# Film values of the modulated stage, made in two earlier stages of a four-layer cross-attention stack

## The chip, the cores and the metric

The kernel runs on one core of one Trainium2 chip. The metric is device time in microseconds (us); a lower one is better. A profile is one execution taken by the hardware profiler. In its rows PE is the tensor engine's matmuls, PEld its weight loads, DVE the vector engine, ACT the scalar engine, POOL the GpSimd engine, and SPq or ACTq a transfer (DMA) that SyncE or ScalarE issues. Every value is f32 unless a row says bf16.

## What is computed

The reference is a stack of four cross-attention layers, each followed by a feed-forward layer, on x of 32 batches x 256 rows x 256 columns and a context ctx of 32 x 120 x 192. The part around the change is in the fourth layer, cut here to what matters:

```python
V = x_vision @ Wv                      # x_vision is ctx; it depends on nothing computed before
c_t = einsum('btg,bgd->btd', attn_mean, V)
scale_in, shift_in = split(c_t @ W_film_in + b_film_in, 2)
...
y = s4d(x, ...)
scale_out, shift_out = split(c_t @ W_film_out + b_film_out, 2)
y = y * (1.0 + mod_gate * scale_out) + mod_gate * shift_out
xt = x_text + y                        # then a layer norm, a gelu feed-forward, a layer norm
```

Since c_t @ W_film_out is attn_mean @ (ctx @ (Wv @ W_film_out)), the kernel folds the two weights once (96 partitions x 2 x 512), makes "film values" of 120 x 512 from a batch's context, and multiplies them with the head weights attn_mean of the batch. ctx, Wv and W_film_out are inputs, so the film values can be made at any time.

## The kernel before

The stages, in the order in which they run, each over the 32 batches:

- a0, `heads_attention`: attention of the first layer. SyncE's queue loads per batch a "floor" of 2 x 960 KB beside the inputs. In its last four batches it also loads what `TernaryHeld` keeps for the next stage.
- one block of five parts that share the engines (`ternary_to_experts`): f0, the ternary feed-forward (`ternary_feed_forward`, tiles f_... and f0w_...); a1, attention; r, the routing; v, `film_rows`, which makes the 32 batches of film values for W_film_in and stores them in the tensor `films`; e, the experts.
- a2, `heads_attention` again, which loads what `AdaptiveHeld` keeps.
- fa, the gated feed-forward with the sparse attention of the fourth layer (`adaptive_with_sparse_attention`, tiles fa_...). It stores attn_mean as `head_weights`.
- cv, the convolution (`convolve_channels`), which loads what `ModulatedHeld` keeps.
- m3, the modulated feed-forward (`modulated_feed_forward`, tiles m_... and m3w_...), and behind it in the same block the low-rank feed-forward.

Between blocks stands a barrier over all engines. Inside a block each engine runs its instructions strictly in the order of the program. That order comes from slots: a part names steps with a lag, and in slot t each engine does, in the order of the list, step(t - lag) for every step whose batch exists. `run_parts` puts several parts side by side: in each slot first all steps of the first part, then those of the next. A part's `first` shifts it, `begin` says in which of its slots `start` runs. So whatever an early list entry waits for holds up everything behind it on that engine.

In f0, VectorE's `start` rounds two weight tiles of 128 x 2048 to ternary values. The mean of their absolute values needs a matmul with ones by TensorE (L1092). Then, for batch i, ScalarE's `norm` runs in slot i+2, TensorE's `turn` and `make_row` in slot i+3, `up` and `conv` in slot i+4 and `turn_max` in slot i+5. VectorE's `h_out` (L1000) empties `up` in slot i+4.

In m3, TensorE's list is `(6, up(0)), (2, film_values), (6, up(1)), (6, up(2)), (2, film_product), (6, up(3)), (5, turn_x), (7, down)`. `start` (L3261) folds the weights; `film_values` (L3270, m_v) makes one batch's values, ScalarE copies them out (L3248, m_vf), and `film_product` (L3279, m_f) multiplies them with the head weights. On VectorE `film_out` makes m_film of it, on POOL `mix` uses m_film.

```python
        def film_values(it):
            pe.wait_ge(c_in[it.p], 16 * (it.h + 1))
            if it.reused(1):
                pe.wait_ge(v_ready, it.i)
            for k in range(2):
                last = pe.matmul(v_ps[0:SK, :], cb[it.p][:, k, :], wvf[:, k, :], start=k == 0, stop=k == 1)
            last.then_inc(v_done, 1)
```

A matmul of this program stands in the trace as two PE instructions, so one batch of film values is x4 there.

Of the kernel before, what the change touches and what calls it, by code (L numbers as in the profile page):

```python
# [15 lines left out]
P = 128  # L16
# [803 lines left out]
def ternary_feed_forward(nc, const, src, dst, held, first, area):  # L820
# [37 lines left out]
    w_scale, w_all, sums, consts = (st.sem(n) for n in ("w_scale", "w_all", "sums", "consts"))  # L858
# [73 lines left out]
    def vector(dve):  # L932

        def start():
            for m, (wq, rows) in enumerate(((w1q, wf[0]), (w2q, wf[1]))):
                dve.tensor_reduce(wsum[:, m:m + 1], rows[:], AX.X, ALU.add, apply_absolute_value=True).then_inc(sums, 1)
                dve.wait_ge(w_all, 4 * m + 1)
                dve.tensor_scalar(wmean[:, m:m + 1], aux[:, 0:1], 1.0 / (D * H1), 1e-5, ALU.mult, ALU.max).then_inc(w_scale, 1)
# [4 lines left out]
                dve.wait_ge(w_all, 4 * m + 2)  # L943
                dve.tensor_scalar(rows[:], rows[:], MAGIC, 1.0, ALU.subtract, ALU.min).then_inc(w_all, 1)
                dve.wait_ge(w_all, 4 * m + 3)
                dve.tensor_scalar(wq[:].rearrange("p k n -> p (k n)"), rows[:], -1.0, 1.0 - 2.0 * m, ALU.max, ALU.mult).then_inc(w_all, 1)

            dve.wait_ge(w_all, 8)
            dve.tensor_reduce(wf[1][:, 0:D], w2q[:].rearrange("p k d -> p d k"), AX.X, ALU.add).then_inc(w_all, 1)
            dve.wait_ge(w_all, 9)  # L950
# [137 lines left out]
    def tensor(pe):  # L1088
        def start():
            for m in two:  # L1090
                pe.wait_ge(sums, m + 1)
                pe.matmul(aux[:, 0:1], const["ones"][:], wsum[:, m:m + 1], start=True, stop=True).then_inc(w_all, 1)  # L1092
            pe.wait_ge(w_all, 10)
# [59 lines left out]
        def down(it):  # L1153
# [11 lines left out]
            (3, make_row(aux, dg, dg_ready, row_done, row_ready)), (5, make_row(aux2, dg2, dg2_ready, row2_done, row2_ready)), (4, conv(1))], 4, start)  # L1165
    after = dict(turned=(turn_ready, B), row=(row_ready, B), hidden=(h_ready, 4 * B), conv=(silu_ready, KH * B), row2=(row2_ready, B), y=(y_ready, B), stored=stored)
# [3 lines left out]
def normed_attention(nc, const, src, dst, ctx, w, first, area, before):  # L1170
# [40 lines left out]
    def sync(sp):  # L1211
        def start():
# [2423 lines left out]
```

## Time and profile before

| | us |
|---|---|
| median of 3 runs | 4773.59 (4771.92 to 4776.9) |
| the profiled execution: its own time | 4771.23 |
| its span, first to last instruction | 4769.5 |
| PE busy | 4437.6 (93%) |
| PEld busy | 3454.4 (72%) |
| DVE busy | 3205.2 (67%) |
| ACT busy | 2043.9 (43%) |
| POOL busy | 2086.4 (44%) |
| mean granted clock of TensorE | 0.974 of full speed |

Busy time is the union of an engine's instructions over the span. Such a share is a mean over stages with different limits, so an edit has to be priced in its own stage: there the question is which engine never waits, and for what the others wait. The granted clock has two levels, 2.4 GHz (1.00 in the rows) and 1.2 GHz (0.50).

### The profile page before, as it was taken

To read this page: it belongs to the slowest core of one execution; us is meant where nothing else is said; L and a number is where in the kernel's file an instruction comes from. 1 tells how busy PE (TensorE), PEld (TensorE's weight loads), DVE (VectorE), ACT (ScalarE), POOL (GpSimd) and SP (SyncE) were. 2 spreads that over 40 slices of the span, in tenths; PEclk is the share of its full clock that TensorE was granted. 3 is DMA by queue.
4 is the path that set the end of the run, shared out by engine and by line. 5 is a ranking of instruction groups with operands and counts; after the bars stand their busy time and mean duration, and the time that the engine had idled before them with its cause. 6 is when DMAs were issued, how large, how long until landed. Compare 5 with 4: busy or idle time off the path is not lost. (4 is left out here: it accounts for less than half of the span.)

```text
span 4769.5 us, 90704 instructions
## 1 busy us (share of the span) xinstructions
PE 4437.6 (93%) x31788; PEld 3454.4 (72%) x31788; DVE 3205.2 (67%) x9688; ACT 2043.9 (43%) x4216; POOL 2086.4 (44%) x2505
## 2 busy tenths in 40 slices
PE   7999869999999999959999899999999978999999
PEld 5666647778776888846666688888888745777866
DVE  5888789987553333147777499999999944444444
ACT  3555447764443232224445344444444332222244
POOL 2222146543444233044443265665655503566532
PEclk9999989999999999979999899999999989999999
DMA  4666612235334322122222111111111073232233
GB/s 112 154 153 163 146 45 70 78 116 182 57 82 100 92 73 71 47 74 69 69 72 89 31 40 34 43 33 34 43 33 32 28 246 130 85 98 84 92 111 102
DMA packets 333274, 407.33 MB, mean 85 GB/s; under 512 B 58932, under 2 KB 294165, under 8 KB 322070
## 3 DMA queue, kind: packets, MB, share of 16 engines
q1 hardware_dynamic: 315190, 368.41, 27.3%
q0 software_dynamic: 13312, 25.25, 2.2%
q10 hardware_dynamic: 4320, 7.87, 0.6%
q8 instruction: 256, 4.19, 0.4%
q14 instruction: 196, 1.61, 0.1%
HBM read 304.45 MB, written 96.96 MB: 84 GB/s over the span
## 5 line engine op out<-in xcount | busy, mean ns | idle before, releaser
L2846 PE MATMUL fa_h<-fa_xnT,faw_w 128*128 128x256 f32 x2048 | 475.1, 383 | 0.0
L2858 PE MATMUL fa_y<-faw_w,fa_hT 128*128 128x256 f32 x2048 | 462.5, 379 | 0.0
L2858 PEld LDWEIGHTS fa_y<-faw_w,fa_hT 128*128 128x128 f32 x2048 | 386.5, 190 | 65.3 <-issue 15.4
L2846 PEld LDWEIGHTS fa_h<-fa_xnT,faw_w 128*128 128x128 f32 x2048 | 380.6, 191 | 56.5 <-issue 9.4
L2743 ACT ACTIVATE fa_hT<-fa_h,faw_b 128x256 f32<-128x256 f32 x512 | 215.0, 471 | 478.0 <-PE fa_h L2846 412.1
L531 DVE TENSOR_REDUCE a_mx<-a_score 128x16 f32<-128x1920 f32 x128 | 276.0, 2157 | 82.2 <-PE a_score L715 81.9
L1966 POOL DMA_INDIRECT e_xg<-moe_rows,e_idx x64 | 128.8, 2013 | 323.8 <-issue 244.7
L3241 ACT ACTIVATE m_hT<-m_h,m3w_b 128x256 f32<-128x256 f32 x256 | 107.5, 471 | 366.5 <-PE m_h L3301 366.5
L1716 PE MATMUL r_h<-r_xnT,r_rw 128*128 128x256 f32 x1024 | 250.1, 393 | 10.7 <-ACT r_hT L1667 10.7
L230 POOL TENSOR_SCALAR a_rs<-a_mv 128x2 f32<-128x2 f32 x96 | 21.4, 223 | 536.9 <-DVE a_mv L224 533.2
L2128 ACT ACTIVATE e_hT<-e_h,e_b 128x256 f32<-128x256 f32 x256 | 107.5, 471 | 329.5 <-PE e_h L2183 319.7
L3301 PE MATMUL m_h<-m_hnT,m3w_w 128*128 128x256 f32 x1024 | 237.5, 381 | 2.5 <-ACT m_hnT L3231 2.5
L3301 PEld LDWEIGHTS m_h<-m_hnT,m3w_w 128*128 128x128 f32 x1024 | 195.1, 191 | 54.2 <-issue 13.6
L2183 PE MATMUL e_h<-e_xT,e_w 128*128 128x256 f32 x1024 | 231.7, 380 | 0.9 <-DVE e_xT L1980 0.9
L2195 PE MATMUL e_y<-e_w,e_hT 128*128 128x256 f32 x1024 | 226.5, 379 | 0.0
L3311 PE MATMUL m_y<-m3w_w,m_hT 128*128 128x256 f32 x1024 | 226.4, 379 | 0.0
L1716 PEld LDWEIGHTS r_h<-r_xnT,r_rw 128*128 128x128 f32 x1024 | 189.6, 193 | 48.2 <-ACT r_hT L1667 23.8
L2195 PEld LDWEIGHTS e_y<-e_w,e_hT 128*128 128x128 f32 x1024 | 194.2, 190 | 26.4
L2183 PEld LDWEIGHTS e_h<-e_xT,e_w 128*128 128x128 f32 x1024 | 191.7, 190 | 25.8 <-DVE e_xT L1980 1.1
L3311 PEld LDWEIGHTS m_y<-m3w_w,m_hT 128*128 128x128 f32 x1024 | 192.1, 190 | 25.2 <-issue 0.4
L765 PE MATMUL a_av<-a_pT,a_vp 120*32 120x256 f32 x2048 | 180.9, 383 | 25.5 <-DVE a_qa L545 24.6
L2669 DVE MATCH_REPLACE8 fa_left<-fa_top,fa_left 128x120 f32<-128x120 f32 x768 | 195.4, 268 | 0.0
(453 smaller groups left out, 11063.3 us busy)
## 6 DMA issues: line engine op xcount, KB each, us to landing
a_floor<-a_lowest SPq DMA_DIRECT2D x64, 960.0 KB
cv_toep<-kernels SPq DMA_DIRECT2D x16, 2048.0 KB, 9.5
x<-a_xo SPq DMA_DIRECT2D x96, 256.0 KB, 3.2
f_xb<-x SPq DMA_DIRECT2D x64, 256.0 KB, 3.2
f_xres<-x SPq DMA_DIRECT2D x64, 256.0 KB, 3.0
a_xb<-x SPq DMA_DIRECT2D x64, 256.0 KB, 3.1
e_w<-in_L_ffn_ew SPq DMA_DIRECT2D x16, 1024.0 KB, 4.8
a_cb<-in_ctx SPq DMA_DIRECT2D x96, 90.0 KB, 2.1
```

What stands on the lines that cost most here:

```text
L531: c.add(dve.tensor_reduce(m, s_in, AX.X, ALU.max))
L765: pe.matmul(av[g * 32:(g + 1) * 32, m * S:(m + 1) * S], vp[it.at][:, (m * G + g) * E + e, :], pT[m][:, g, h * S:(h + 1) * S], start=h == 0 ...
L1716: last = pe.matmul(h_ps[m % 2][:, c, :], rw1[:, k, f:f + P], xnT[it.p][:, k, :], start=k == 0, stop=k == KD - 1)
L1966: pool.indirect_dma_start(xg[p][:, t, :], None, xn_all[:, :], bass.IndirectOffsetOnAxis(ap=idx[p][:, t:t + 1], axis=0), bounds_check=B * S ...
L2183: last = pe.matmul(h_ps[m][:, c, :], w1[e][:, k, f:f + P], xT[it.p][:, k, :], start=k == 0, stop=k == KD - 1)
L2195: last = pe.matmul(y_ps[it.p][:, t * D:(t + 1) * D], hT[it.p][:, k, t * P:(t + 1) * P], w2[e][:, k, :], start=k == 0, stop=k == KH - 1)
L2669: c.add(dve.match_replace(left[t][:, h, :], top[t][:, rnd, h, :], rows[:, h, :], TAKEN))
L2743: act.activation(hT[e % 2][:, 2 * m + c, :], h_ps[j % 2][:, c, :], ACT.Relu, bias=b1[:, f:f + 1]).then_inc(h_ready, 1)
L2846: last = pe.matmul(h_ps[j % 2][:, c, :], w1[:, e, k, f:f + P], xnT[it.p][:, k, :], start=k == 0, stop=k == KD - 1)
L2858: last = pe.matmul(bank[:, t * D:(t + 1) * D], hT[e % 2][:, k, t * P:(t + 1) * P], w2[:, e, k, :], start=k == 0, stop=k == KE - 1)
L3301: last = pe.matmul(h_ps[m % 2][:, c, :], w1[:, k, f:f + P], hnT[it.p][:, k, :], start=k == 0, stop=k == KD - 1)
L3311: last = pe.matmul(y_ps[:, t, :], hT[it.p][:, k, t * P:(t + 1) * P], w2[:, k, :], start=k == 0, stop=k == KH - 1)
```

## The change

The 32 batches of film values for W_film_out are no longer made in m3. `film_rows` is generalised and used twice. As new part "u" it stands directly behind the ternary part in the list, with first = -3 and counts (4, 4, 2, 0, 0, 0, 6, 6). So it folds the weights in slot -4, makes ten batches in slots -3 to -1, and six each in slots 3 and 4, behind the ternary part's own steps. It stores the fold as `film_fold` and the values as `films_out`. The last ten batches are made in the last two slots of fa, three and seven of them, ahead of the other steps. m3 now loads 240 KB of finished values per batch in place of 90 KB of context.

```diff
-    COUNT = 4
+    COUNT, FILMS = 11, 22
...
     def load(self, sp, part, done):
+        b = slice(part * self.FILMS // 4, (part + 1) * self.FILMS // 4)
+        sp.dma_start(self.cb[:, b], self.ctx[b].rearrange("b c k s -> c b k s")).then_inc(done, 16)
...
+        if part == 3:
+            for a, n in ((self.film_wv, "Wv"), (self.film_wf, "W_film_out")):
+                sp.dma_start(a[:], self.v[n]).then_inc(done, 16)
...
         def start():
+            for m in two:
+                dve.tensor_reduce(wsum[:, m:m + 1], wf[m][:], AX.X, ALU.add, apply_absolute_value=True).then_inc(sums, 1)
+            dve.wait_ge(summed, 2)
             for m, (wq, rows) in enumerate(((w1q, wf[0]), (w2q, wf[1]))):
-                dve.tensor_reduce(wsum[:, m:m + 1], rows[:], AX.X, ALU.add, apply_absolute_value=True).then_inc(sums, 1)
-                dve.wait_ge(w_all, 4 * m + 1)
...
         def turn_max(it):
             pe.wait_ge(pmax_ready, it.i + 1)
+            if it.i == 0:
+                pe.wait_ge(*films["ready"])
...
+        def rows(it):
+            for b in range(firsts[it.i], firsts[it.i] + counts[it.i]):
                 if b == 0:
                     pe.wait_ge(fold_ready, 2)
...
                 if b >= 2:
                     pe.wait_ge(v_ready, b - 1)
                 for k in range(2):
                     last = pe.matmul(banks[b % 2][0:SK, :], cb[:, b, k, :], wvf[:, k, :], start=k == 0, stop=k == 1)
                 last.then_inc(v_done, 1)
...
+    u, _, u_after, film_out = film_rows(nc, const, "u", ctx, films_out, kw, "W_film_out", False, -3, (4, 4, 2, 0, 0, 0, 6, 6), (5, 7),
+                                        Area((at, mid)), held, folds)
...
+            sp.dma_start(self.wvf[:], self.folds).then_inc(done, 16)
+            sp.dma_start(self.late[:], self.ctx).then_inc(done, 16)
...
+    late = {B - 2: range(0, 3), B - 1: range(3, LATE)}
...
+            def late_values(it):
+                for j in late.get(it.i, ()):
+                    if j == 0:
+                        pe.wait_ge(h_ready, 2 * PAIRS * B)
+                    if j >= 2:
+                        pe.wait_ge(lv_ready, j - 1)
+                    for k in range(2):
+                        last = pe.matmul(h_ps[j % 2][0:SK].rearrange("p c s -> p (c s)"), held.late[:, j, k, :], held.wvf[:, k, :], start=k == 0, stop=k == 1)
+                    last.then_inc(lv_done, 1)
...
             pipeline(pe, B, DEPTH, [
-                (4, difficulty), (5, up(0)), (4, gates), (5, up(1)), (5, up(2)), (5, up(3)), (6, turn_sum),
+                (7, late_values), (4, difficulty), (5, up(0)), (4, gates), (5, up(1)), (5, up(2)), (5, up(3)), (6, turn_sum),
...
-            sp.dma_start(cb[it.p][:], ctx[it.i]).then_inc(c_in[it.p], 16)
+            sp.dma_start(vf[it.p][:], films[it.i]).then_inc(v_in[it.p], 16)
             sp.dma_start(aT[it.p][:], at_all[it.i]).then_inc(a_in[it.p], 16)
...
-        return Program([(6, up(0)), (2, film_values), (6, up(1)), (6, up(2)), (2, film_product), (6, up(3)), (5, turn_x), (7, down)], 2, start)
+        return Program([(6, up(0)), (6, up(1)), (6, up(2)), (2, film_product), (6, up(3)), (5, turn_x), (7, down)], 2)
```

ScalarE copies each batch of values out of the bank and issues its store: in "u" it follows the counts of TensorE, in fa the copies stand first in the slot and SyncE's queue stores them. In part v (W_film_in) the fold moves one slot earlier. The loads of W_film_out and Wv (512 and 192 KB) leave the end of cv and go to the end of a0.

TensorE at the beginning of the ternary stage, before (f_aux<-f_wsum is the sum of weights, f_qt_ps `turn`, f_h_ps `up`, f_c_ps `conv`):

```order
L1092 MATMUL f_aux<-f_wsum,c_ones 128x1 x2
L1102 MATMUL f_qt_ps<-c_identb,f_qx_7079 128x128 x4
L1112 MATMUL f_aux<-f_dg_7083,c_ones 128x128 x2
L1125 MATMUL f_h_ps<-f_qxT_7081,f_w1q 128x256 x8
L1140 MATMUL f_c_ps<-f_hs_7091,f_diag 64x256 x24
L1125 MATMUL f_h_ps<-f_qxT_7081,f_w1q 128x256 x8
L1102 MATMUL f_qt_ps<-c_identb,f_qx_7080 128x128 x4
L1112 MATMUL f_aux<-f_dg_7084,c_ones 128x128 x2
L1140 MATMUL f_c_ps<-f_hs_7091,f_diag 64x256 x24
L1125 MATMUL f_h_ps<-f_qxT_7082,f_w1q 128x256 x8
```

And the same place in the changed kernel (u_bank is a bank of film values, x20 are ten batches):

```order
L1860 MATMUL u_bank<-f0w_wf,f0w_wv 96x512 x4
L1102 MATMUL f_aux<-f_wsum,c_ones 128x1 x2
L1872 MATMUL u_bank<-u_wvf,f0w_cb 120x512 x20
L1114 MATMUL f_qt_ps<-c_identb,f_qx_7095 128x128 x4
L1124 MATMUL f_aux<-f_dg_7099,c_ones 128x128 x2
L1872 MATMUL u_bank<-u_wvf,f0w_cb 120x512 x12
L1137 MATMUL f_h_ps<-f_qxT_7097,f_w1q 128x256 x8
L1152 MATMUL f_c_ps<-f_hs_7107,f_diag 64x256 x24
L1137 MATMUL f_h_ps<-f_qxT_7097,f_w1q 128x256 x8
L1114 MATMUL f_qt_ps<-c_identb,f_qx_7096 128x128 x4
L1152 MATMUL f_c_ps<-f_hs_7107,f_diag 64x256 x24
L1137 MATMUL f_h_ps<-f_qxT_7098,f_w1q 128x256 x8
```

Ten batches of values stand between the sum of weights and the first `turn`, and six between the first row and the first `up`. Six more stand between the last `conv` piece of the first batch and the `up` of the second batch (left out of the rows, since they read as the six before).

TensorE in the steady part of the modulated stage, before (m_h `up`, m_v `film_values`, m_f `film_product`, m_t `turn_x`, m_y `down`):

```order
L3301 MATMUL m_h<-m_hnT_51050,m3w_w_49729 128x256 x4
L3270 MATMUL m_v<-m_wvf,m_cb_51052 120x512 x2
L3301 MATMUL m_h<-m_hnT_51050,m3w_w_49729 128x256 x8
L3279 MATMUL m_f<-m_vf,m_aT_51054 128x512 x2
L3288 MATMUL m_t<-c_ident,m_xn_51023 128x128 x4
L3311 MATMUL m_y<-m3w_w_49730,m_hT_51058 128x256 x16
```

After:

```order
L3337 MATMUL m_h<-m_hnT_51352,m3w_w_50034 128x256 x12
L3315 MATMUL m_f<-m_vf_51354,m_aT_51356 128x512 x2
L3337 MATMUL m_h<-m_hnT_51352,m3w_w_50034 128x256 x4
L3324 MATMUL m_t<-c_ident,m_xn_51325 128x128 x4
L3347 MATMUL m_y<-m3w_w_50035,m_hT_51359 128x256 x16
```

The m_v row is gone, and the first three quarters of `up` follow each other directly.

## Rows read from the trace of the kernel before

**Rows 1.** Windows, modulated stage; columns: length, PE, PEld, DVE, ACT, POOL, PEclk, DMA, GB/s.

```profile
4200.00:4300.00 100.00, 100.00 (x430) 79.45 (x429) 41.71 (x127) 26.67 (x61) 58.91 (x68) 1.00 0.28 85
```

**Rows 2.** Timeline, PE, steady modulated stage: start, duration, instruction, count.

```profile
4204.32 1.89 PE L3301 MATMUL m_h<-m_hnT,m3w_w 128*128 128x256 f32 x8
4206.05 1.88 PE L3270 MATMUL m_v<-m_wvf,m_cb 96*120 96x512 f32 x4
4207.77 3.62 PE L3301 MATMUL m_h<-m_hnT,m3w_w 128*128 128x256 f32 x16
```

**Rows 3.** Chain that ended last, beginning of the modulated stage: start, duration, what.

```profile
3962.00 5.09 PE m_f L3261 x8
...
3970.40 2.00 PE m_f L3279 x4
...
3984.23 2.65 DMA m_cb<-in_ctx
...
3986.93 1.99 PE m_v L3270 x4
...
3989.58 3.78 PE m_f L3279 x4
```

**Rows 4.** Timeline, PE, beginning of the ternary stage (in brackets: idle before, and releaser).

```profile
634.18 0.58 PE L1102 MATMUL f_qt_ps<-c_identb,f_qx 128*128 128x128 bf16 x4 [14.35 <-DVE f_qx L991]
...
636.17 1.89 PE L1125 MATMUL f_h_ps<-f_qxT,f_w1q 128*128 128x256 bf16 x8 [0.39 <-ACT f_qxT L1053]
640.80 4.24 PE L1140 MATMUL f_c_ps<-f_hs,f_diag 64*64 64x256 f32 x48 [2.74 <-DVE f_hs L1000]
...
646.96 2.82 PE L1140 MATMUL f_c_ps<-f_hs,f_diag 64*64 64x256 f32 x48 [0.22 <-DVE f_hs L1000]
649.71 1.05 PE L1125 MATMUL f_h_ps<-f_qxT,f_w1q 128*128 128x256 bf16 x8
```

**Rows 5.** Timeline, ACT, beginning of the ternary stage.

```profile
630.58 1.09 ACT L1047 ACTIVATE f_xn<-f_xb,f_minus,f_rs 128x256 f32<-128x256 f32 x2 [34.14 <-DVE f_minus L960]
```

**Rows 6.** Timeline, DVE, beginning of the ternary stage.

```profile
609.63 2.29 DVE L936 TENSOR_REDUCE f_wsum<-f0w_wf 128x1 f32<-128x2048 f32 x1 [5.78 <-PEq L205]
612.60 0.16 DVE L938 TENSOR_SCALAR f_wmean<-f_aux 128x1 f32<-128x1 f32 x1 [0.68 <-PE f_aux L1092]
...
639.48 1.26 DVE L1000 TENSOR_TENSOR f_hs<-f_h_ps,f_row 128x512 f32<-128x512 f32 x2
...
650.43 1.29 DVE L1000 TENSOR_TENSOR f_hs<-f_h_ps,f_row 128x512 f32<-128x512 f32 x2 [0.66 <-PE f_h_ps L1125]
```

**Rows 7.** Windows, ternary stage: the first weights, and the steady part.

```profile
610.00:620.00 10.00, 1.18 (x4) 1.01 (x4) 8.50 (x8) 0.00 (x0) 9.33 (x25) 0.50 0.34 106
...
680.00:700.00 20.00, 19.55 (x257) 14.29 (x259) 19.47 (x40) 15.59 (x26) 13.55 (x10) 1.00 0.20 67
```

**Rows 8.** Timeline, PE, part v: its first four batches of values.

```profile
1507.50 7.13 PE L1841 MATMUL v_bank<-v_wvf,v_cb 96*120 96x512 f32 x16 [0.67 <-ACT v_wvf L1802]
```

**Rows 9.** Lines of ScalarE in part v: copies and stores (min/median/max ns).

```profile
L1814 ACT ACTIVATE v_vf<-v_bank,v_mod x32: 667/687/689, 1509.5 to 1567.4; 120x512 f32<-120x512 f32 x32
L1806 ACTq DMA_DIRECT2D films<-v_vf x32: 322/323/598, 1511.2 to 1568.1; - x32
```

**Rows 10.** Timeline, PE, last two slots of the gated stage.

```profile
3805.01 1.12 PE L2809 MATMUL fa_t<-c_ident,fa_xn 128*128 128x128 f32 x4 [6.38 <-DVE fa_xn L238]
...
3817.86 3.78 PE L2905 MATMUL fa_ba<-fa_vf,fa_aT 121*128 121x512 f32 x4 [0.46 <-ACT fa_aT L2789]
3834.99 0.47 PE L2896 MATMUL fa_ba<-c_ident,fa_mean 128*120 128x128 f32 x1 [13.36 <-DVE fa_mean L2701]
...
3837.02 3.78 PE L2905 MATMUL fa_ba<-fa_vf,fa_aT 121*128 121x512 f32 x4 [0.46 <-ACT fa_aT L2789]
```

**Rows 11.** First attention: window of its last loads; who waited for the floor.

```profile
460.00:480.00 20.00, 18.70 (x217) 13.37 (x210) 16.77 (x20) 9.51 (x16) 4.13 (x5) 1.00 0.87 219
...
  DMA a_floor<-a_lowest: 2.7, 1
```

More of the change, by code:

```diff
@@ L1212, in start @@
         def start():
+            for done, n in before["films"]:
+                sp.wait_ge(done, n)
             for a, n in ((wq, "Wq"), (wk, "Wk"), (wv, "Wv"), (wo, "Wo")):
@@ L1798, in fold_out @@
         def fold_out():
-            act.wait_ge(weights, 48)
+            if not held:
+                act.wait_ge(weights, 48)
             for m in range(2):
@@ L1813, in step @@
                     act.wait_ge(kept[b % FOUR], 16 * (b // FOUR))
-                act.activation(vf[b % FOUR][:], banks[b % 2][0:SK, :], ACT.Copy, scale=mod[0:SK, 0:1]).then_inc(v_ready, 1)
+                act.activation(vf[b % FOUR][:], banks[b % 2][0:SK, :], ACT.Copy, **COPY).then_inc(v_ready, 1)
                 if b:
                     keep(b - 1)
-            return step
         def finish():
-            keep(B - 1)
-        return Program([(0, rows_out(j)) for j in four], start=fold_out, begin=0, finish=finish)
+            keep(n - 1)
+            if folds is not None:
+                act.wait_ge(folds_kept, 16)
+        return Program([(0, rows_out)], start=fold_out, begin=-1, finish=finish)
     def tensor(pe):
         def fold():
-            pe.wait_ge(weights, 48)
+            if not held:
+                pe.wait_ge(weights, 48)
             for m in range(2):
@@ L1830, in fold @@
                 last.then_inc(folded, 1)
-        def rows(j):
-            def step(it):
-                b = FOUR * it.i + j
+        def rows(it):
+            for b in range(firsts[it.i], firsts[it.i] + counts[it.i]):
                 if b == 0:
                     pe.wait_ge(fold_ready, 2)
-                    pe.wait_ge(c_in, 16 * FOUR)
+                if not held and b % (B // FOUR) == 0:
+                    pe.wait_ge(c_in[b * FOUR // B], 16)
                 if b >= 2:
@@ L1842, in step @@
                 last.then_inc(v_done, 1)
-            return step
-        return Program([(0, rows(j)) for j in four], start=fold, begin=0)
-    return st, late, dict(ready=(v_ready, B), kept=[(kept[p], 16 * B // FOUR) for p in four]), Part(
-        first, B // FOUR, 1, sync, gpsimd, vector, scalar, tensor)
+        return Program([(0, rows)], start=fold, begin=-1)
+    return st, late, dict(ready=(v_ready, n), kept=[(kept[p], 16 * len(range(p, n, FOUR))) for p in four]), Part(
+        first, len(counts), 1, sync, gpsimd, vector, scalar, tensor)
 def experts(nc, const, xn_all, table, eo, w, kpad, kw, first, area, over_routing, over_films, before, films):
@@ L2331, in adaptive_with_sparse_attention @@
     GT = 256
+    vl = [st.sb(f"vl{p}", [SK, 2 * D]) for p in range(4)]
     assert nc.sbuf_base <= held.low
+    lv_done, lv_ready = st.sem("lv_done"), st.sem("lv_ready")
+    lv_kept = [st.sem(f"lv_kept{p}") for p in range(4)]
     wready, padded = st.sem("wready"), st.sem("padded")
@@ L2423, in _ @@
             sp.wait_ge(aT_kept, 16 * B)
+            for p in range(4):
+                sp.wait_ge(lv_kept[p], 16 * len(range(p, LATE, 4)))
         @block.gpsimd
@@ L3278, in film_product @@
             for t in range(TL):
-                last = pe.matmul(f_ps[t][:], aT[it.p][:, t * P:(t + 1) * P], vf[:], start=True, stop=True)
+                last = pe.matmul(f_ps[t][:], aT[it.p][:, t * P:(t + 1) * P], vf[it.p][:], start=True, stop=True)
             last.then_inc(f_done, 1)
@@ L3458, in narrow @@
             pe.wait_ge(xT_ready, it.i + 1)
-            if it.i == 0:
-                pe.wait_ge(*before["values"])
             if it.reused(1):
```

175 lines of the change are left out of this document (90 added, 85 removed).

## The prediction

> **What bounds the kernel now.** I read the windows by stage first, then the timeline of the engines where instructions leave or arrive, then the chain of waits at the stages' ends. A window row gives, behind its length, the busy time of PE, PEld, DVE, ACT and POOL, each with its count.
>
> The stage that loses work is bound by TensorE without a gap: in 100 us PE is busy 100.00, VectorE 41.71, ScalarE 26.67, POOL 58.91, at full clock, and the DMA engines 28% [rows 1]. The stage that receives 22 batches is another kind. In its steady part VectorE (19.47 of 20 us) and PE (19.55) both hardly rest [rows 7]. Its beginning is VectorE's: for 14.35 us before the first `turn` TensorE does nothing but wait [rows 4], since VectorE starts on the weights at 609.63 [rows 6], and the clock stands at 0.50 [rows 7]. The end of the gated stage is VectorE's too: PE waits 6.38 and 13.36 us in its last two slots [rows 10].
>
> **The term that leaves, modulated stage.** A batch of values takes TensorE from 4206.05 to 4207.77, 1.72 us [rows 2]. It stands next to `up` for batches 4 to 31 (slots 6 to 33), where PE never waits: 28 x 1.72 = 48.2 us. Would another engine take over? A batch is 76 PE instructions (32 m_h, 32 m_y, 4 each of m_v, m_f and m_t), so the 430 of [rows 1] are 5.65 batches of 17.7 us, and without m_v one needs 16.0. Of that POOL needs 10.4 us, VectorE 7.4, ScalarE 4.7. The first three quarters of `up` now stand back to back, so the third waits for the two gelus of the first. All of ScalarE's work for a batch is 4.7 us, so two of eight gelus are below 1.2 us, and the second quarter gives them 1.73 us (4204.32 to 4206.05 for one quarter [rows 2]). No new wait; if I am wrong by 0.3 us a batch, 9 us are missing.
>
> In the fill, batches 1 and 2 lie beside POOL and count nothing; two places count. First, from the fold's start at 3962.00 to the first m_f at 3970.40 [rows 3], 8.4 us of fold, copy, values and copy. In their place the first m_f waits for its own transfers. The 90 KB one took 2.65 us [rows 3]; for 240 KB and the 120 KB of weights issued behind it I take 3.5 us (bounds 2.65 and 5). The fold also raised the clock; without it the m_f matmuls take 3.78 us as at 3989.58 and not 2.00 [rows 3]. That leaves 8.4 - 3.5 - 1.8 = 3.1 us. Second, from m_v at 3986.93 to m_f at 3989.58, 2.65 us, less 0.8 for the longer transfer ahead of it: 1.8 us. Sum of the stage: 48.2 + 3.1 + 1.8 = 53.1 us, bounds 44 and 57.
>
> A rule speaks against this. PE's matmul row is busy 100.00 us of 100, but the weight loads (PEld) only 79.45 [rows 1]. The Trainium skill, "Perfetto Trace Analysis", section "Identifying the Most-Contended Engine", says that matmul busy time is a bad measure of how near TensorE is to its limit, and that weight-load busy time is a better one. By it a fifth of these 1.72 us would be slack that was there anyway, and the term 28 x 1.37 = 38.4 us. I go by the start times instead: the row behind m_v starts when m_v's 1.72 us are over. The other reading is a rival below.
>
> **What arrives, beginning of the ternary stage.** Four pieces, all in PE's strict order.
> The fold goes ahead of the sum of weights. At a cold start it took 5.09 us [rows 3], so it ends near 614.7. VectorE's two reductions of 2.29 us end at 614.2 [rows 6], and its two waits of 0.68 us become one. Together that is nothing, up to 1.8 us if the clock rises later.
> Ten batches follow, at 7.13 us for four in the warm case [rows 8], which is 1.78 each with the last one's drain and 1.72 without. ScalarE's copy (0.69) and store (0.32) [rows 9] fit under that with two banks. They start near 615.8, behind the second fold's copy, and end at 633.0. Their cover is VectorE's work on the weights; it ends too soon. ScalarE must copy the tenth before `norm`, which began at 630.58 [rows 5] and now begins at about 633.8: 3.2 us lost.
> Six batches, 10.3 us, stand between `turn` and the first `up` (636.17 [rows 4]). VectorE took that `up` only at 639.48 [rows 6], from a PE that ended it at about 638.1, so 1.4 us are covered. A warm `up` gives 0.8 back, and clock lost while PE waits for `turn` may take 1.7. I count 8.0. The conv of the first batch then runs warm: 2.82 in place of 4.24 us, 1.4 back [rows 4].
> Six more stand between the second conv piece (646.96) and the second `up` (649.71) [rows 4]. There VectorE waited 0.66 us for PE already [rows 6]. Nothing covers them: 10.3 us. What is late next is every `h_out` after it, and VectorE has no rest later to catch up [rows 7].
> Sum: 3.2 + 8.0 - 1.4 + 10.3 = 20.1 us lost, bounds 13 and 28. The wait of `turn_max` for all 22 costs nothing: they stand ahead of it in order.
>
> **What arrives, end of the gated stage.** Three batches, 5.2 us, lie in the 6.38 us of waiting before 3805.01. Seven batches, 12.0 us warm, begin when the products before them end, at 3821.6, and so end at about 3833.7, or 3835.5 if the first is cold; `mean_heads` comes at 3834.99 [rows 10]. Their cover is 13.36 us of PE waiting; without it they would cost 17.2. They leave the clock up, so the last product takes 2.0 and not 3.78 us [rows 10]: 1.3 us gained, bounds -3 and +3. On SyncE's queue seven stores go ahead of the last head weights, which are ready later than they.
>
> **Loads and small things.** a0 takes about 0.5 MB more in each of its last four load slots, and 0.7 MB of weights in the last. At 219 GB/s 0.5 MB is 2.3 us. The DMA engines were already busy 87% there, so some 2.2 us of a batch's 17 were free. VectorE waited for the floor only once, 2.7 us in 64 [rows 11]. I take 1 us, bounds 0 and 10. Part v: its wait of 0.67 us behind the fold goes [rows 8]. The loads that leave cv and those that join a2 count nothing (bounds -2 and 1 us), as cv is followed by compute anyway. Sum of these: 0.3 lost.
>
> **Sum.** 53.1 + 1.3 - 20.1 - 0.3 = 34.0 us. The profiled execution took 4771.23 us and would take 4737.2; its span is 4769.5. The median of the runs is 4773.59, 2.4 above, which gives 4739.6.
>
> **The rivals.** Differences below 0.2% (9.5 us) are about what a measurement of this kernel can't tell from none.
> 1. *Hidden anyway*: the twelve batches of slots 3 and 4 fall into waits of PE that I underrate. For it: 2.74 and 0.39 us of idle stand between the first rows [rows 4]; against it: that is 3 us against 20.6. It would cost 4 us instead of 20: 4723. Chance 0.07.
> 2. *Less comes back*: the slack reading above, or a wait of `up` for gelu that replaces m_v. For it: PEld 79.45 [rows 1]; against it: the start times. 10 us less: 4750. Chance 0.08.
> 3. *The floor is late*: the extra transfers push SyncE's small store of the floor's source, and the floor, behind VectorE's clip. For it: 87% busy. 4 to 10 us: 4744 to 4750. Chance 0.12 for over 5 us.
> 4. *Slower than before*: TensorE's clock stays at 0.50 through the values, as it stood in this stretch [rows 7]. A batch then costs 3.57 us (3.78 less the overlap), 22 batches 40.7 us more and the fold 1.8: 34.0 - 42.5 = -8.5, so 4782. It decides from 3.26 us a batch. Against it: the clock rose within m3's fold, 5.09 us for eight instructions where four cold ones take 3.78 [rows 3], and v's batches ran at 1.78 [rows 8]. A part of it, the first few batches after each wait, gives 4743 to 4755. Chance 0.04 for the whole, 0.10 for a part.
> 5. *No change that can be told*: rivals 2 and 3 together with a cold part. 4764 to 4783. Chance 0.04.
>
> **How the numbers follow.** My own forecast, 4731 to 4748, has 0.55. The single time is its centre, 4739.6. The range reaches up over rivals 2, 3 and the cold part of 4, and down over half of 1: 4727 to 4757. Faster by more than 0.2%: 0.55 + 0.07 + 0.08 + 0.12 + 0.10 = 0.92; within 0.2%: 0.04 and half of rival 4, 0.06; slower: 0.02.
>
> **What would show it.** In the modulated stage m_v is gone and a batch takes 16.0 us, PE at 100% and no ScalarE wait before `up`. The first m_f starts about 3.5 us behind the stage's start. In the ternary stage `norm` starts 24.2 us behind the first reduction (before 20.95), the second `up`'s `h_out` 61 us behind it (before 40.8). In the gated stage the last `mean_heads` stands where it did. I am wrong if values take over 2 us each in the ternary stage, if `h_out` is less than 15 or more than 27 us later, if VectorE waits for a_floor in a0's last slots, or if PE shows gaps between quarters of `up`.

## The result, and the profile after

The changed kernel takes 4739.06 us (median of 4 runs, 4731.56 to 4745.7) beside 4775.24 us for the kernel before on the same chip: ratio 0.9929, interval 0.9915 to 0.9942, 36 us less. A second comparison gave 0.9915 (0.9901 to 0.9928). The profiled execution took 4731.56 us with a span of 4729.8 us (before 4769.5).

Timeline of PE, VectorE (DVE) and ScalarE (ACT) in the profile after, beginning of the ternary stage; they answer to [rows 4, 6].

```profile
608.00 5.49 PE L1860 MATMUL u_bank<-f0w_wf,f0w_wv 128*96 128x512 f32 x8 [6.39 <-PEq L205]
608.00 4.48 DVE L945 TENSOR_REDUCE f_wsum<-f0w_wf 128x1 f32<-128x2048 f32 x2 [5.67 <-PEq L205]
...
614.16 17.43 PE L1872 MATMUL u_bank<-u_wvf,f0w_cb 96*120 96x512 f32 x40 [0.33 <-ACT u_wvf L1829]
...
632.11 1.08 ACT L1057 ACTIVATE f_xn<-f_xb,f_minus,f_rs 128x256 f32<-128x256 f32 x2
633.23 0.69 DVE L979 TENSOR_REDUCE f_amax<-f_xn 128x2 f32<-128x512 f32 x1 [3.38 <-ACT f_xn L1057]
...
637.10 11.42 PE L1872 MATMUL u_bank<-u_wvf,f0w_cb 96*120 96x512 f32 x24
...
648.36 1.04 PE L1137 MATMUL f_h_ps<-f_qxT,f_w1q 128*128 128x256 bf16 x8
...
649.08 1.29 DVE L1010 TENSOR_TENSOR f_hs<-f_h_ps,f_row 128x512 f32<-128x512 f32 x2 [7.99 <-PE f_h_ps L1137]
...
650.42 2.82 PE L1152 MATMUL f_c_ps<-f_hs,f_diag 64*64 64x256 f32 x48 [1.02 <-DVE f_hs L1010]
...
653.83 1.29 DVE L1010 TENSOR_TENSOR f_hs<-f_h_ps,f_row 128x512 f32<-128x512 f32 x2 [2.67 <-PE f_h_ps L1137]
...
669.03 1.29 DVE L1010 TENSOR_TENSOR f_hs<-f_h_ps,f_row 128x512 f32<-128x512 f32 x2 [11.05 <-PE f_h_ps L1137]
```

The reader is to see three waits of VectorE that grew: 3.38 us for ScalarE's `norm`, 7.99 us for the first `up`, 11.05 us for the second batch's `up`. Counted from the first reduction (609.63 before, 608.00 after), `norm` starts at 24.11 (before 20.95), the first `h_out` at 41.08 (29.85), its second piece at 45.83 (35.98) and the second batch's at 61.03 (40.80). The delay is 3.2, 11.2, 9.9 and 20.2 us.

Windows of the modulated stage, answering to [rows 1], and PE's timeline over one steady batch.

```profile
4200.00:4300.00 100.00, 100.00 (x455) 83.50 (x454) 51.28 (x137) 27.32 (x64) 65.98 (x77) 1.00 0.35 109
```

```profile
4160.56 5.34 PE L3337 MATMUL m_h<-m_hnT,m3w_w 128*128 128x256 f32 x24
4165.74 1.88 PE L3315 MATMUL m_f<-m_vf,m_aT 120*128 120x512 f32 x4
4167.47 1.89 PE L3337 MATMUL m_h<-m_hnT,m3w_w 128*128 128x256 f32 x8
4169.19 0.60 PE L3324 MATMUL m_t<-c_ident,m_xn 128*128 128x128 f32 x4
4169.63 7.07 PE L3347 MATMUL m_y<-m3w_w,m_hT 128*128 128x256 f32 x32
4176.54 3.83 PE L3337 MATMUL m_h<-m_hnT,m3w_w 128*128 128x256 f32 x17
```

No row carries a wait, the three quarters of `up` follow each other, and a batch takes 4176.54 - 4160.56 = 15.98 us. The stage's beginning:

```profile
3981.71 3.75 PE L3315 MATMUL m_f<-m_vf,m_aT 120*128 120x512 f32 x4 [10.00 <-DMA m_aT<-head_weights]
3987.06 3.75 PE L3315 MATMUL m_f<-m_vf,m_aT 120*128 120x512 f32 x4 [1.59 <-DVE m_film L3257]
...
4005.97 5.45 PE L3337 MATMUL m_h<-m_hnT,m3w_w 128*128 128x256 f32 x24 [1.11 <-ACT m_hnT L3293]
...
4025.87 4.48 PE L3347 MATMUL m_y<-m3w_w,m_hT 128*128 128x256 f32 x20
```

The first m_f comes 3.7 us behind the stage's first instruction (3977.99) and runs at 1.2 GHz.

The gated stage's last slots, answering to [rows 10]:

```profile
3818.39 5.32 PE L2971 MATMUL fa_h<-faw_wvf,faw_late 96*120 96x512 f32 x12
3824.94 0.66 PE L2865 MATMUL fa_t<-c_ident,fa_xn 128*128 128x128 f32 x4 [1.23 <-DVE fa_xn L238]
...
3840.82 12.18 PE L2971 MATMUL fa_h<-faw_wvf,faw_late 96*120 96x512 f32 x28
3854.47 0.33 PE L2952 MATMUL fa_ba<-c_ident,fa_mean 128*120 128x128 f32 x1 [1.47 <-DVE fa_mean L2750]
...
3856.33 1.98 PE L2961 MATMUL fa_ba<-fa_vf,fa_aT 121*128 121x512 f32 x4 [0.46 <-ACT fa_aT L2838]
```

Waits of 6.38 and 13.36 us became 1.23 and 1.47 us, filled with values, and the last product takes 1.98 us in place of 3.78.

**The span in stretches.** Every profile of the study, cut at the same instructions (us): A, from the span's start to the first reduction; B, to the last `h_out` of f0; C, to the first turn (e_t) of the experts; D, to VectorE's last work in the experts; E, to the first load of the second attention; F, to POOL's first work in the gated stage; G, to the last turn_sum; H, to the first matmul of the convolution; I, to the modulated stage; K, to the end. "To" an instruction means to its start. Their sum is the span, to 0.2 us.

| kernel | A | B | C | D | E | F | G | H | I | K |
|---|---|---|---|---|---|---|---|---|---|---|
| before | 609.6 | 394.1 | 563.4 | 472.5 | 17.6 | 601.4 | 1147.0 | 43.3 | 113.0 | 807.5 |
| after | 608.0 | 414.3 | 564.6 | 472.5 | 18.0 | 602.9 | 1145.1 | 41.7 | 111.0 | 751.7 |
| e1_both | 610.1 | 414.5 | 566.5 | 472.5 | 16.8 | 602.6 | 1146.9 | 43.0 | 111.9 | 805.3 |
| e2_no_values | 610.9 | 394.2 | 567.2 | 472.5 | 17.5 | 603.4 | 1145.6 | 43.3 | 112.8 | 751.5 |
| e3_ten | 611.3 | 398.1 | 561.3 | 472.5 | 18.0 | 602.9 | 1145.2 | 41.7 | 109.6 | 752.3 |
| e4_no_late | 609.9 | 415.4 | 568.5 | 472.5 | 16.8 | 601.7 | 1146.4 | 43.1 | 111.4 | 752.9 |
| e5_again | 612.1 | 414.9 | 560.1 | 472.5 | 18.0 | 598.4 | 1147.1 | 41.7 | 111.1 | 751.5 |
| e6_spread | 608.8 | 415.3 | 563.0 | 472.5 | 18.0 | 600.5 | 1145.8 | 41.7 | 110.8 | 751.8 |
| e7_gated | 614.3 | 409.9 | 559.1 | 472.5 | 18.3 | 599.2 | 1151.7 | 41.9 | 111.3 | 752.0 |
| e8_tail | 610.9 | 401.4 | 547.7 | 472.5 | 30.7 | 600.8 | 1147.0 | 43.0 | 110.3 | 752.5 |
| e9_twelve | 614.6 | 412.1 | 560.8 | 472.5 | 16.5 | 601.3 | 1145.4 | 41.7 | 111.0 | 751.7 |
| e10_store | 611.1 | 415.7 | 555.3 | 472.5 | 11.9 | 601.6 | 1146.6 | 41.7 | 110.8 | 751.9 |
| e11_tail_store | 610.6 | 401.3 | 558.0 | 472.5 | 26.4 | 601.2 | 1146.1 | 42.4 | 112.5 | 752.3 |
| e12_all | 609.4 | 407.7 | 564.6 | 472.5 | 12.2 | 601.3 | 1149.0 | 41.9 | 113.7 | 752.6 |

### The profile page after: what moved, and what is told of

Its sections match the earlier page's. It is cut to its first block and busy times, and to the rows that moved or that the text cites. A ratio compares the mean times of both kernels' runs of the same rounds, so it can differ in the third digit from the quotient of the medians.

```text
span 4729.8 us, 90726 instructions
## 1 busy us (share of the span) xinstructions
PE 4425.8 (94%) x31788; PEld 3448.2 (73%) x31788; DVE 3222.4 (68%) x9688; ACT 2041.2 (43%) x4216; POOL 2072.9 (44%) x2505
## 5 line engine op out<-in xcount | busy, mean ns | idle before, releaser
L230 POOL TENSOR_SCALAR a_rs<-a_mv 128x2 f32<-128x2 f32 x96 | 21.4, 222 | 536.5 <-DVE a_mv L224 533.8
L2225 PEld LDWEIGHTS e_y<-e_w,e_hT 128*128 128x128 f32 x1024 | 194.2, 190 | 26.4
```

What stands on the lines that cost most here:

```text
L2225: last = pe.matmul(y_ps[it.p][:, t * D:(t + 1) * D], hT[it.p][:, k, t * P:(t + 1) * P], w2[e][:, k, :], start=k == 0, stop=k == KH - 1)
```

## The experiments

The first four kernels shared a chip and 9 runs of the kernel before (4772.14 us), the next four 11 runs (4768.26), the last four 9 runs (4776.72). So medians are compared by their ratio to before. A ratio's interval is about 0.0014 to either side, 7 us; smaller things are read from the stretches, of which there is one profile for each kernel.

**e1_both: only the costs.** m3 as before the change, beside the early values.

```diff
-            sp.dma_start(vf[it.p][:], films[it.i]).then_inc(v_in[it.p], 16)
+            sp.dma_start(cb[it.p][:], ctx[it.i]).then_inc(c_in[it.p], 16)
...
+        return Program([(6, up(0)), (2, film_values), (6, up(1)), (6, up(2)), (2, film_product), (6, up(3)), (5, turn_x), (7, down)], 2, start)
```

Expected:

> The early values are made and stored as in the changed kernel, but the modulated stage is that of the kernel before: it folds the weights and makes all 32 batches of values itself, and the early ones are not used. So this kernel holds only the costs of the change. My theory (the work moved costs its TensorE time in the beginning of the ternary stage, 20.1 us, and next to nothing in the gated drain and in the loads): the time before plus 18 to 22 us, near 4794. Rival, the loss is mostly elsewhere (loads, floor) and the ternary part is hidden: the h_out behind the second up comes less than 10 us later than before, and the time is before plus 5 to 12. Rival, m3 did not give 53 us but something else did: then this kernel stays below before plus 10.

Measured: 4794.93 us, ratio 1.0046 (1.0033 to 1.006), 22.8 us above before. B is 414.5 against 394.1: 20.4 of it lie in the ternary stage. The gain is m3's: K is 805.3 here.

**e2_no_values: only the gain.** The kernel before, whose m3 is that of the changed kernel and reads `films`.

```diff
-            sp.dma_start(cb[it.p][:], ctx[it.i]).then_inc(c_in[it.p], 16)
+            sp.dma_start(vf[it.p][:], films[it.i]).then_inc(v_in[it.p], 16)
...
-        return Program([(6, up(0)), (2, film_values), (6, up(1)), ...
+        return Program([(6, up(0)), (6, up(1)), ...
```

Expected:

> The kernel before, with the modulated stage of the changed kernel: it makes no film values for W_film_out and folds nothing, and reads the stored values of W_film_in in their place (so the film values of W_film_out are left out). No value is made early. It holds only the gain of the change. My theory: 28 x 1.72 + 3.1 + 1.8 = 53.1 us by the prediction, 55.7 us by the stage's length in the trace of the changed kernel, so 4719 to 4722 where before takes 4775. Rival, less comes back because the weight loads or the gelus keep TensorE at its pace: 35 to 45 us below before, 4730 to 4740.

Measured: 4721.49 us, ratio 0.9893 (0.9878 to 0.9909), 50.7 us below before; K is 751.5, 55.9 less. All stretches ahead of I are those of before within 4 us. The slack of the weight loads that PEld 79.45 [rows 1] seemed to offer wasn't there: a batch got 17.70 - 15.98 = 1.72 us shorter, not 1.37, and PEld's share rose to 83.50. What a row took in PE's order is what its removal gave. The price of 1.37 us was the prediction's own reading of the Trainium skill, "Perfetto Trace Analysis", section "Identifying the Most-Contended Engine", which judges there how near TensorE is to its limit and prices no edit.

By the medians the two halves add up to 50.7 - 22.8 = 28 us, 8 to 12 less than the whole change gave in its two comparisons. The three intervals allow about that much. In the profiles most of it lies in C and F, where these two kernels together are 10 us longer than before and the changed kernel 3. The same two stretches differ by 9 us between the two profiles of the changed kernel (e5_again below).

**e3_ten and e9_twelve: the two groups of the ternary stage apart.** First without the twelve of slots 3 and 4, then without the ten ahead of the first turn.

```diff
-    u, _, u_after, film_out = film_rows(..., False, -3, (4, 4, 2, 0, 0, 0, 6, 6), (5, 7),
+    u, _, u_after, film_out = film_rows(..., False, -3, (4, 4, 2, 0, 0, 0, 0, 0), (5, 7),
```

```diff
-    u, _, u_after, film_out = film_rows(..., False, -3, (4, 4, 2, 0, 0, 0, 6, 6), (5, 7),
+    u, _, u_after, film_out = film_rows(..., False, -3, (0, 0, 0, 0, 0, 0, 6, 6), (5, 7),
```

Expected:

> The changed kernel without the twelve batches of values in slots 3 and 4 of the ternary stage (they are left out; the modulated stage reads values of batches 0 to 9 for batches 10 to 21). My theory: these twelve batches lie in TensorE's order where VectorE waits for up, with 8.0 and 10.3 us of cost less 1.4 us that a warm conv gives back, so 16.9 us less than the changed kernel, 4739 - 17 = 4722, and the ratio to before near 0.989. Rival, hidden anyway: the twelve cost 4 us or less, and the time is 4735 or more.

> The changed kernel without its first ten batches of values in the ternary stage (left out; the modulated stage reads those of batches 0 to 9 from batches of slots 3 and 4). The fold and the twelve of slots 3 and 4 stay. My theory: the ten cost only that norm is 3.2 us late, so norm is back at 21 us behind the first reduction, the last h_out comes 16 to 17 us later than in the kernel before instead of 20.2, and the time is 3 to 4 us below the changed kernel. Rival: the ten also keep TensorE's clock up for what follows; without them turn, the six of slot 3 and the first up run at half clock (a batch 3.57 us and not 1.72), and the last h_out comes 20 us or more later, as in the changed kernel.

Measured: e3_ten 4719.55 us, ratio 0.9891 (0.9876 to 0.9906); B 398.1, so the ten cost 4.0 us alone and the twelve 16.2 to 17.6 beside them (B was 414.3 to 415.7 in the six profiles with all 22). e9_twelve 4729.61 us, ratio 0.9909 (0.9895 to 0.9923); `norm` 21.4 us behind the reduction, B 412.1, 17.9 above before where 16 to 17 were expected: beside the twelve the ten cost 2.2 to 3.6 us. Without them the first `h_out` comes 17.4 us behind `norm` and not 17.0, and the six of slot 3 take 11.81 us, within the 11.42 to 12.99 of the profiles that have all 22. "Hidden anyway" falls, and so does the rival of a clock that only the ten hold up. The median can't tell e9_twelve from the changed kernel (0.9915); the stretch can.

**e4_no_late: the gated drain.**

```diff
-    late = {B - 2: range(0, 3), B - 1: range(3, LATE)}
+    late = {}
```

Expected:

> The changed kernel without the ten batches of values in the last two slots of the gated stage (left out; the modulated stage reads the values of batches 0 to 9 for batches 22 to 31). The loads of their contexts stay. My theory: they cost nothing, since TensorE waited 6.4 and 13.4 us there, and they keep the clock up, so the last film product takes 2.0 us in place of 3.8: without them the time is 1 to 4 us longer than that of the changed kernel, and the stretch from the last turn_sum to the modulated stage is 157 us long again as in the kernel before, where the changed one has 153. Rival, the stretch got shorter for another reason (the loads that left the convolution): then it stays at 153 to 154, and the time is that of the changed kernel or 1 us below.

PE's rows at the same place:

```profile
3860.47 0.47 PE L2950 MATMUL fa_ba<-c_ident,fa_mean 128*120 128x128 f32 x1 [13.36 <-DVE fa_mean L2748]
...
3862.48 3.62 PE L2959 MATMUL fa_ba<-fa_vf,fa_aT 121*128 121x512 f32 x4 [0.46 <-ACT fa_aT L2836]
```

Measured: 4740.27 us, ratio 0.9932 (0.9918 to 0.9946). The wait of 13.36 us is back and the last product slow again; H is 43.1 against 41.7. So ten values cost nothing and give 1.4 us. They give it only where the clock stays up: in the changed kernel the granted clock is 1.00 from 3856 to 3858, at the last product; in e1_both the values were made too, yet the clock was 0.50 from 3861 to 3863, the product took 3.78 us, and H was 43.0. H + I is 154.5 us here and not the 157 that was expected, 152.7 in the changed kernel, 156.3 before. The 1.8 us between here and before lie in I, but for 0.2; the rival puts them down to the loads that left the convolution, which no run shows, since I spreads by more than that between kernels with the same loads.

**e5_again: the changed kernel once more,** for the 14 us between its runs.

Expected:

> The changed kernel once more, for its spread: its four runs lay 14 us apart (4731.6 to 4745.7), those of the kernel before 6 us. My theory: the spread is not in the stages that the change touches. The four profiles so far, all of them with the same program from the last h_out of the ternary part to the beginning of the gated stage, differ by 6 us there and by 3 us or less in any other stage. So in this profile the ternary part's last h_out comes 414.3 us behind the first reduction, the modulated stage takes 751.7 (both within 1), and what differs in length lies between them or in the first attention. Rival, the new values or loads sit on an edge that falls differently from run to run (floor, clock): then one of these two numbers, or the 608 us of the first attention, moves by over 3 us.

Measured: 4728.46 us (4722.81 to 4732.86), ratio 0.9915. B 414.9 and K 751.5 stand within 0.6 us of the first profile; C and F are 4.5 us shorter each, A is 4.1 longer. Over all 14 profiles C lies between 547.7 and 568.5 and A between 608.0 and 614.6, while B in the six profiles with all 22 values and K in the twelve without `film_values` in m3 repeat to 1.4 us. Of B's 1.4 us most is the six values of slot 3, which take 11.42 us in the first profile and 12.99 in that of e10_store. Runs of the kernel before lie 14 to 16 us apart as well, with more of them (4767.74 to 4781.8, 4760.49 to 4776.2). What spreads stretch C, the routing above all, was not tried. A moved by over 3 us, as the rival said, but its parts tell where. From the norm of batch 28 to that of batch 31, where the new loads lie, A takes 51.1 us in the kernel before and in e2_no_values, and 52.0 to 54.3 in the seven kernels with all new loads at A's end (mean 53.1). The rest of A's spread lies ahead of batch 4 (75.3 to 78.8 us) and behind the last norm (70.0 to 73.8), in kernels with and without the loads.

**e6_spread: the loads of the first attention, earlier.**

```diff
+                if clip and B - 12 <= it.i < B - 4 and it.i % 2:
+                    held.early((it.i - (B - 12)) // 2, sp, held_in)
```

Expected:

> The changed kernel with the contexts for the ternary stage loaded in batches 20, 22, 24 and 26 of the first attention in place of its last four, where weights are loaded too. My theory: the loads cost at most 1 us where they are (the first attention took 608.0 to 611.3 us in all kernels, with and without them), so the time stays within 2 us of the changed kernel. Rival, the floor is late: VectorE waited 6.6 us for it in the changed kernel and 2.7 in the one before; then the wait goes back to 2.7 us and the kernel gains 3 to 4 us.

Measured: 4729.34 us, ratio 0.9917 (0.9903 to 0.9931), not to be told from 0.9915. Batches 28 to 31 take 51.1 us again, as in e12_all. Who waited for the floor, changed kernel and then e6_spread:

```profile
DVE a_pT L554 <- DMA a_floor<-a_lowest: 6.6, 4, 3.7
```

```profile
DVE a_pT L556 <- DMA a_floor<-a_lowest: 3.6, 1, 3.6
```

Of the changed kernel's four waits one stands in the first slots, at 50.7 us, where the kernel before has its only one. The other three are new and lie in the last slots (0.6 us before 496.9, 0.6 before 531.7, 1.6 before 587.9). In e6_spread these three are gone and the 3.6 us are the wait of the first slots. So the floor was late, as the rival said, and at the end of A the loads cost 2.0 us on average (53.1 - 51.1), 1.5 in the changed kernel: more than the 1 us expected, less than the rival's 3 to 4. Earlier they cost nothing that shows.

**e7_gated: four values to the first slot of the gated stage,** counts (4, 4, 2, 0, 0, 0, 4, 4).

```diff
+                (0, first_values), (3, first_emptied), (7, late_values), (4, difficulty), (5, up(0)), ...
```

Expected:

> Four of the twelve batches of values of slots 3 and 4 are moved to the first slot of the gated stage, where TensorE waited 5 us and more for VectorE at half clock. All values are made. My theory: two batches less stand in each of the slots 3 and 4, so the ternary part gets 6.9 us shorter; in the gated stage four cold batches take 4 x 3.6 = 14 us less what they cover (5 to 10 us), so it gets 0 to 5 us longer, and the sum is 2 to 7 us below the changed kernel, 4732 to 4737. Rival, they raise the clock there and cost nothing: 7 us. Rival, the cold batches and their context delay the first turn by their full length: 3 us above.

Measured: 4726.42 us, ratio 0.9906 (0.9892 to 0.992). B is 409.9, 5 us shorter; G is 1151.7 against 1145.1 to 1147.1, 4.6 to 6.6 longer. The idle time at that place covers little: the values begin with the stage at 2673.43 and take 10.58 us, and the first turn stands behind them at 2684.69, 11.3 us behind POOL's first work, where in the changed kernel it stands 3.4 us behind. The sum by stretches is about nothing, less than the 2 to 7 us expected.

**e8_tail: eight values to the end of the experts' block,** counts (4, 4, 2, 0, 0, 0, 4, 0).

```diff
+def tail_rows(nc, ctx, films, folds, before, base, n, places, first, area):
...
-    run_parts(nc, [ternary, film_out, attention, routing, film, expert])
+    run_parts(nc, [ternary, film_out, attention, routing, film, expert, tail])
```

Expected:

> Eight of the twelve batches of values of slots 3 and 4 are moved to the end of the experts part: four stay in slot 3, none in slot 4. At the end of that block TensorE ends at 2059.4 us, and the barrier opens at 2077.4, since the last store of the kernels lands then. All values are made; their contexts and the folded weights are loaded some twenty slots earlier. My theory: TensorE's time in the ternary part is a cost because nothing covers it there; 8 x 1.72 = 13.8 us go from it, and at the block's end 13.8 us + 0.7 copy + 2.4 store = 16.9 us lie inside the 18 us of waiting. So 12 to 14 us below the changed kernel, 4725 to 4727. Rival, the stores of values and the small packets of the kernels' store share the DMA engines and the barrier opens later by 3 to 8 us: 4730 to 4736. Rival, what was lost in the ternary part comes back elsewhere anyway (the parts behind it have slack): no gain, 4739.

Measured: 4724.93 us, ratio 0.9912 (0.9899 to 0.9926). B is 13 us shorter, as expected, and E 12.7 us longer. The timeline of that end:

```profile
2032.27 10.46 PE L1926 MATMUL w_bank<-w_wvf,w_cb 96*120 96x512 f32 x24
...
2044.43 0.59 ACT L1906 COPY w_vf<-w_bank 120x512 f32<-120x512 f32 x1 [4.51 <-DMA films_out<-w_vf]
...
2045.07 5.39 PE L1926 MATMUL w_bank<-w_wvf,w_cb 96*120 96x512 f32 x8 [2.34 <-ACT w_vf L1906]
...
2063.17 0.33 SPq L379 DMA_DIRECT2D a_wq<-in_L_xattn_Wq  x1
```

The values' stores are slow beside the kernels' small packets (4.51 us of waiting for a buffer). That is the first rival, but it explains 4.3 of the 12.7 us: with the kernels' store out of the way E is 26.4 and not 30.7 (e11_tail_store). The rest came out of the next two.

**e10_store and e11_tail_store: the kernels' store early,** in the changed kernel and in e8_tail.

```diff
-        return Program([(0, load_index), (0, load_weights), (6, store)], UNROLL, start, -EARLY, finish)
+        return Program([(0, load_index), (0, load_weights), (6, store)], UNROLL, start, -EARLY, finish, {N: store_kernels})
```

Expected (the parenthesis in the first on 2.4 MB is a slip: the stores are of 128 and 256 KB):

> The changed kernel with one thing that the change does not touch: the store of the convolution kernels (2.4 MB-free tail: 128 and 256 KB in packets under 512 bytes) is issued some 70 us before the end of the experts part, where its source is finished, and not behind the last store of the experts. My theory: the block's barrier waited for it alone (last VectorE work at 2059.4 us, barrier at 2077.4), so the barrier opens 3 to 4 us behind VectorE's last work and the kernel gains 13 to 15 us, near 4714 to 4716 against 4728 for the changed kernel in the last comparison. Rival: the wait is the barrier's own or the small packets hold up the gathers and stores of the last experts instead: 0 to 5 us.

> The kernel with eight batches of values moved to the end of the experts part, with the early store of the kernels as in the run before. With the store late the barrier opened 30.7 us behind VectorE's last work in place of 18.0, which ate the gain. My theory: values' stores and the small packets of the kernels' store held each other up; with the latter gone the values take 13.8 us, a copy and a store 3.1, and the barrier opens 17 us behind. So against the same kernel with the late store 13 to 14 us less, and 0 to 2 us more or less than the changed kernel with the early store, since TensorE's 13.8 us are then not covered at either place. Rival: the values' stores are slow by themselves (over 5 us each), and the barrier opens over 22 us behind.

Measured: e10_store 4726.42 us, ratio 0.9906 (0.9889 to 0.9922), E 11.9 and not 4; e11_tail_store 4725.22 us, ratio 0.9896 (0.9881 to 0.9911), E 26.4 and not 17. Both expectations fail, by 8 and by 9 us. Windows of e10_store, VectorE's last work being at 2054.6 (DMA share and GB/s are the last two columns):

```profile
2055.00:2057.00 2.00, 0.00 (x0) 0.00 (x0) 0.27 (x1) 0.00 (x0) 0.00 (x0) 1.00 0.35 131
2057.00:2059.00 2.00, 0.00 (x0) 0.00 (x0) 0.00 (x0) 0.00 (x0) 0.00 (x0) 0.79 0.00 0
...
2063.00:2065.00 2.00, 0.00 (x0) 0.00 (x0) 0.00 (x0) 0.00 (x0) 0.00 (x0) 0.50 0.00 0
2065.00:2067.00 2.00, 0.00 (x0) 0.00 (x0) 0.45 (x5) 0.00 (x0) 0.52 (x3) 0.50 0.00 0
```

The last transfer is over by 2057, and the next block begins at 2066.5. In the changed kernel the same stretch lies behind the small packets:

```profile
2064.00:2066.00 2.00, 0.00 (x0) 0.00 (x0) 0.00 (x0) 0.00 (x0) 0.00 (x0) 0.50 0.49 63
2066.00:2068.00 2.00, 0.00 (x0) 0.00 (x0) 0.00 (x0) 0.00 (x0) 0.00 (x0) 0.50 0.15 18
2068.00:2070.00 2.00, 0.00 (x0) 0.00 (x0) 0.00 (x0) 0.00 (x0) 0.00 (x0) 0.50 0.00 0
```

Its next block begins at 2077.4. So some 9 to 10 us between the last transfer and the next block belong to the block's end itself. What fills them stands in e10_store's trace, SyncE's queue from 2055 to 2067:

```profile
L204 SPq EVENT_SEMAPHORE_RANGE_CLEAR  x145: 25/25/49, 2057.8 to 2066.2; - x145
```

The row gives the count, the shortest, median and longest duration in ns, and the first and last start. Line 204 is in the kernel's own `end_all`, which clears every semaphore of the block's stages, one instruction for each, ahead of the barrier that all engines wait at. The 145 clears take 8.4 of the 9.5 us, about 58 ns from one start to the next. The kernel before has 132 here and 9.1 us, e11_tail_store 147 and 9.9 us. Two other block ends of the changed kernel have 50 in 2.7 us and 54 in 3.4 us. No run clears fewer, so what that would save was not tried.

Of the 18 us in E only 8.5 are cover, where the expectations had counted them all, and 6.1 of these are the kernels' own late store (18.0 - 11.9). With that, e11_tail_store comes out by its own rows: the values end 13.7 us behind the start of VectorE's last work, the last copy takes 0.6, its store 2.2, the end 9.9: 26.4.

**e12_all: e6, e7 and e10 together.**

Expected:

> Three pieces together: four batches of values in the first slot of the gated stage, the contexts loaded in batches 20 to 26 of the first attention, and the early store of the kernels. My theory: 2.9 us (6.9 less 4.0 by the profiles) + 1.5 us (the last batches of the first attention took 51.1 us with the loads moved and 52.6 with them at the end) + 13 to 15 us: 17 to 20 us below the changed kernel, 4708 to 4711 against 4728. Rival: the pieces overlap or only the store counts: 4714.

Measured: 4722.29 us (4716.35 to 4726.55), ratio 0.9886 (0.9871 to 0.9901): 54 us below before, the lowest ratio here of a kernel that computes all. Its interval just touches that of e5_again (0.9901 to 0.9928) and overlaps that of e11_tail_store. By the stretches about 12 us are gained on the changed kernel: B 7, E 6, the loads 2, less some 3 in G. That is less than the 17 to 20 expected, since the early store gives 6 us and not 13 to 15.

## Why the prediction was right

4739.6 us was forecast and 4739.06 measured. That the two agree to 0.6 us is luck: four runs lay 14 us apart, and in the second comparison the same program's median was 4728.46. The difference to before is the fairer measure: 34.0 us was forecast, the two comparisons gave 36 and 40, and the profiles 39.7. The terms that the prediction names measured 55.7 + 1.6 - 20.2 - 1.5 = 35.6 us by the two profiles; the other 4 us lie in stretches that spread as much between kernels with the same work there. By its own terms:

- **Modulated stage, 53.1 us.** 55.7 by the two profiles, 53.6 against e1_both, whose m3 is the same program as that of before. The 2.2 us between those two lie in the fill: the first `up` ran at 1.2 GHz in the profile of before (3.78 us for x8), at 2.4 GHz in e1_both (1.99). In the changed kernel it ran at 2.4 GHz too, and the prediction had no term for that. From the stage's start to the first `up` it forecast 4.9 us less; 5.4 was measured against before, 4.0 against e1_both. The steady term, 28 x 1.72, is right: 17.70 to 15.98 a batch. The first m_f was forecast 3.5 us behind the start, and came at 3.7.
- **Ternary stage, 20.1 us.** 20.2. Each piece held: `norm` 3.2 (3.2), six values in slot 3 8.0 (8.1), conv 1.4 back (1.4), six in slot 4 10.3 (10.4). e3_ten and e9_twelve show what each group costs alone, 4.0 and 17.9 us, 1.7 more in sum than together. The clock didn't fall to 1.2 GHz for whole groups: the 22 values ran at 1.74 to 1.90 us each (17.43 for ten, 11.42 and 10.56 for six). The one slower group, 11.42, is some 1 us of it, and it is 1.6 us more in e10_store (12.99), so that this agreement to 0.1 us is in part luck as well.
- **Gated drain, 1.3 us.** 1.6 in H of the changed kernel, 0.3 in e1_both. Right in mechanism, but it hangs on the clock, and the 1.3 was less than the 1.8 that its two durations, 3.78 and 2.0, give.
- **Loads, 1 us.** 1.5 us in the changed kernel (52.6 - 51.1), 2.0 on average. The prediction had named it as a sign of being wrong if VectorE waited for a_floor in a0's last slots, and it did wait there, three times, 2.8 us in sum. So the mechanism of rival 3 is there, at a size below the rival's. The convolution's end, counted at nothing, is 2 us shorter in the changed kernel, but that this is the loads isn't shown: I is 113.0 and 111.9 in the two kernels that load W_film_out and Wv there (before and e1_both), and 109.6 to 113.7 in the twelve others.
- **Rivals.** 1 falls with e3_ten, 2 with e2_no_values, 3 happened, at some 2 us and not 4 to 10, 4 didn't occur, 5 needed them.

What stays open is why stretch C differs by 4.5 us between two runs of one program, and by up to 21 us (547.7 to 568.5) between kernels.

## What to carry to other kernels

Work that any time can hold is worth moving only to where its engine waits: 28 x 1.72 us left a full stage, the ten in the gated stage's drain cost nothing where TensorE waited for VectorE, and the twelve that stood ahead of what VectorE waits for cost 1.35 to 1.47 of their 1.72 us each. Where an engine's order is strict, the price of a row is the difference of start times around it, not its share of some other unit. And a gap ahead of a barrier is not all cover: take off what the block's end takes for itself. It shows as the stretch in which neither engines nor transfers are busy, and it is worth asking the sequencer's rows for what fills it: here one clear for each of 145 semaphores.

## What the runs showed of the hardware that was not expected

- Between the last transfer of the experts' data and the first instruction of the next 9.5 to 9.9 us pass in which no engine computes (e10_store 2057.0 to 2066.5, the changed kernel 2067.9 to 2077.4, e11_tail_store 2058.9 to 2068.8). SyncE clears 145 to 147 semaphores there one by one, at 58 to 60 ns each, and the other engines wait at the barrier behind that. The only transfer in between is one of 8 KB on an instruction queue (4 GB/s from 2059 to 2061 in e10_store).
- Two stores of 384 KB in all, 256 KB of it in 4096 packets of 64 bytes, kept the DMA engines at about half for some 6 us, at 63 to 82 GB/s, where the values' stores by themselves moved 123 to 175 GB/s at a share of 0.46 to 0.60 (e11_tail_store, 2046 to 2058). The Trainium skill, "DMA: Bandwidth & Descriptors", section "Why small descriptors are slow (HBM only)", names a fixed overhead for each packet; the rows agree in direction.
- The same instructions behind the same wait run at either clock in different executions (first `up` of the modulated stage, the same program in both kernels: 3.78 us in before and 1.99 us in e1_both for x8), which moves a stage's fill by 2 us.
